# A graph network's edge stage on one core: raw edge features transposed two tiles at a time and split behind the transposes, with ScalarE's steps in another order

## What is computed

```python
ei = jnp.concatenate([x[src], edge_attr], axis=-1)          # 100000 x (256 + 64)
core = jnp.maximum(ei @ W1 + b1, 0.0) @ W2 + b2
gate = jax.nn.sigmoid(ei @ Wg + bg)
agg = jax.ops.segment_sum(gate * core, dst, num_segments=N)
out = agg + x
# layer norm of out; x = layernorm(x + out); then two hops of a normalised
# neighbour sum, a 256x256 product, log-softmax, and a last layer norm
```

## Time and profile before

| | us |
|---|---|
| median of 3 runs | 2623.61 (2621.59 to 2627.11) |
| the profiled execution | 2622.07 |
| its span, first to last instruction | 2620.1 |
| TensorE busy, share of the span | 2366.6, 90% |
| VectorE busy | 1906.3, 73% |
| ScalarE busy | 1638.6, 63% |
| GpSimd busy | 1417.6, 54% |

### The profile page before, as it was taken

One profiled execution on the slowest core, in us unless ns is written; L12 is line 12 of the kernel. 1 busy time (PEld: TensorE's weight loads), 2 busy tenths in 40 slices (PEclk: granted clock), 3 DMA queues, 4 the chain that ended last, 5 costly groups with the idle time before them and its releaser, 6 DMA issues. The chain is left out here.

```text
span 2620.1 us, 48396 instructions
## 1 busy us (share of the span) xinstructions
PE 2366.6 (90%) x16053; PEld 1842.6 (70%) x16053; DVE 1906.3 (73%) x4579; ACT 1638.6 (63%) x3119; POOL 1417.6 (54%) x1385
## 2 busy tenths in 40 slices
PE   7879999999999999999999994799999999888864
PEld 3469999999999999999999992255555444445443
DVE  6647777777777777888888999896777851435455
ACT  1158888888888888888888884464676630102123
POOL 0265555555555555555555641466666626666663
PEclk9989999999999999999999996899999999999986
DMA  6555555555555556556666652354565445565542
GB/s 209 194 182 166 167 164 164 164 164 164 164 166 163 165 164 179 174 163 180 179 179 181 179 152 82 86 147 130 134 170 149 114 141 192 183 217 191 168 131 87
DMA packets 276156, 422.40 MB, mean 161 GB/s; under 512 B 127618, under 2 KB 198548, under 8 KB 273860
## 3 DMA queue, kind: packets, MB, share of 16 engines
q0 software_dynamic: 90368, 281.11, 37.7%
q1 hardware_dynamic: 170028, 116.99, 14.6%
q10 hardware_dynamic: 15512, 21.17, 2.3%
HBM read 354.78 MB, written 64.37 MB: 160 GB/s over the span
## 5 line engine op out<-in xcount | busy, mean ns | idle before, releaser
L823 POOL DMA_INDIRECT gathered<-p_table,src_t x784 | 793.0, 1012 | 621.4 <-PE banks L965 431.6
L823 POOL DMA_INDIRECT gathered<-hop_table,src_t x576 | 591.5, 1027 | 437.4 <-issue 148.3
L988 PE MATMUL banks<-w_hi,hidden_hi 128*128 128x256 f32 x1568 | 458.0, 292 | 30.4 <-ACT banks L1327 29.6
L988 PE MATMUL banks<-w_lo,hidden_hi 128*128 128x256 f32 x1568 | 442.6, 282 | 0.0
L988 PE MATMUL banks<-w_hi,hidden_lo 128*128 128x256 f32 x1568 | 442.1, 282 | 0.0
L1440 ACT CAST counts<-banks 128x686 f32 (+3 forms) x382 | 295.5, 773 | 174.4 <-PE banks L1053 76.3
L1320 ACT CAST msg_hi<-room 128x512 fp32r<-128x512 f32 x392 | 242.1, 618 | 213.0 <-DVE room L1810 207.7
L1810 DVE TENSOR_TENSOR room<-banks,gate 128x512 f32<-128x512 f32 x392 | 255.9, 686 | 153.3 <-issue 122.9
L988 PEld LDWEIGHTS banks<-w_hi,hidden_hi 128*128 128x128 f32 x1568 | 297.6, 190 | 48.7 <-issue 38.1
L1800 DVE SCALAR_TENSOR_TENSOR hidden_lo<-banks,hidden_hi 128x512 fp32r<-128x512 f32 x392 | 268.7, 689 | 55.5 <-ACT hidden_hi L1313 32.8
L1050 PE MATMUL banks<-codes,low_hot 128*128 128x343 f16 (+3 forms) x958 | 240.3, 335 | 74.8 <-DVE codes L2026 47.9
(11 more groups left out here) (223 smaller groups left out, 5249.1 us busy)
## 6 DMA issues: line engine op xcount, KB each, us to landing
ea<-in_edge_attr SPq DMA_DIRECT2D x196, 128.0 KB
counts_saved<-counts SPq DMA_DIRECT2D x16, 1568.0 KB
ring<-counts_saved SPq DMA_DIRECT2D x16, 1568.0 KB
gathered<-p_table,src_t POOLq DMA_INDIRECT x784
p_table<-p_t ACTq DMA_DIRECT2D x48, 256.0 KB, 3.4
hop_table<-parts SPq DMA_DIRECT2D x12, 896.0 KB
gathered<-hop_table,src_t POOLq DMA_INDIRECT x576
x_saved<-x_room SPq DMA_DIRECT2D x7, 896.0 KB
```

What stands on the lines that cost most here:

```text
L823: pool.indirect_dma_start(out=rows[:, n % slots, j, :], out_offset=None, in_=table[:, :], in_offset=bass.IndirectOffsetOnAxis(ap=src_t[:, ...
L988: last = nc.tensor.matmul(banks[:, 4 + half, j % 2 * H:(j % 2 + 1) * H], lhs, rhs, start=False, stop=n == len(products) - 1, skip_group_ch ...
```

## The change

- TensorE transposes the raw features, two tiles side by side (2 x 64 columns), so two transposes for a group, not four. They wait for the load itself (`ea_loaded`). In bank 7, partitions 0 to 63 then hold tiles 0 and 2, partitions 64 to 127 tiles 1 and 3.
- ScalarE's `round_ea` and `copy_ea` go. `upper_ea(n+3)` makes the upper parts in two copies of 64 partitions x 256 out of the bank, and VectorE's `lower_ea`, now at lag 3, makes the lower parts in two subtractions of 64 x 256, out of the bank and into the 64 partitions opposite. It raises `ea_ready`.
- Tiles stand in another order in the transposed table (`turned_at`). `load_ea` waits for `ea_turned`, not for `ea_split`.
- ScalarE's order: open_gate goes from the end of the step to just behind upper_ea and the node rows, one group later (lag 1, not 2); seed_core is taken apart: half 0 stands between upper_msg half 0 and upper_hidden 0, half 1 closes the step.

```diff
+        def turned_at(j):
+            return slice((j % 2 * 2 + j // 2) * P, (j % 2 * 2 + j // 2 + 1) * P)
+        raw_halves = ((slice(0, DE), slice(0, 2 * P), slice(DE, P)), (slice(DE, P), slice(2 * P, GROUP), slice(0, DE)))
             def load_ea(i, s):
-                wait_count(sp, S["ea_split"], g - 1)
+                wait_count(sp, S["ea_turned"], g - 1)
             def turn_ea(turn, s, g):
-                pe.wait_ge(S["ea_split"], g + 1)
+                pe.wait_ge(S[f"ea_loaded{s}"], 16 * (turn + 1))
                 wait_count(pe, S["ea_ready"], g)
-                for j in range(TILES):
-                    last = nc.tensor.transpose(banks[:, 7, j * P:(j + 1) * P],
-                                               ea_split[:, s, j, :, :].bitcast(F32).rearrange("p b d -> p (b d)"), ident[:, :])
+                for j in range(TILES // 2):
+                    last = nc.tensor.transpose(banks[:, 7, j * P:(j + 1) * P], ea[:, s, 2 * j:2 * j + 2, :].rearrange("p b d -> p (b d)"), ident[:, :])
-            def round_ea(turn, s, g):
-                act.wait_ge(S[f"ea_loaded{s}"], 16 * (turn + 1))
-                wait_count(act, S["ea_turned"], g - 1)
-                nc.scalar.copy(ea_split[:, s, :, 0, :], ea[:, s, :, :]).then_inc(S["ea_rounded"], 1)
-            def copy_ea(turn, s, g):
+            def upper_ea(turn, s, g):
                 act.wait_ge(S["ea_turned"], g + 1)
                 wait_count(act, S["gate_product"], 2 * (g - 1))
-                nc.scalar.copy(ea_turned_sb[:, s, :], banks[:, 7, :]).then_inc(S["ea_ready"], 1)
+                for rows, columns, _ in raw_halves:
+                    nc.scalar.copy(ea_turned_sb[rows, s, columns], banks[rows, 7, 0:2 * P]).then_inc(
+                        S["ea_upper"], 1)
             def step(i, s, in_order=True):
-                at_group(copy_ea, i, s, 3)
-                at_group(round_ea, i, s, 5)
+                at_group(upper_ea, i, s, 3)
                 if in_order and isinstance(i, int):
                     node_rows_at(2 * i + s)
+                at_group(open_gate, i, s, 1)
                 at_group(seed_gate, i, s, 2)
                 at_group(upper_msg(0), i, s, 0)
+                at_group(seed_core(0), i, s, 1)
                 at_group(upper_hidden(0), i, s, 2)
                 at_group(upper_msg(1), i, s, 0)
                 at_group(upper_hidden(1), i, s, 2)
-                at_group(seed_core, i, s, 1)
-                at_group(open_gate, i, s, 2)
+                at_group(seed_core(1), i, s, 1)
             def lower_ea(turn, s, g):
-                dve.wait_ge(S["ea_rounded"], g + 1)
-                nc.vector.tensor_tensor(ea_split[:, s, :, 1, :], ea[:, s, :, :], ea_split[:, s, :, 0, :].bitcast(F32),
-                                        ALU.subtract).then_inc(S["ea_split"], 1)
+                for half, (rows, columns, others) in enumerate(raw_halves):
+                    dve.wait_ge(S["ea_upper"], 2 * g + half + 1)
+                    last = nc.vector.tensor_tensor(ea_turned_sb[others, s, columns], banks[rows, 7, 0:2 * P],
+                                                   ea_turned_sb[rows, s, columns].bitcast(F32), ALU.subtract)
+                last.then_inc(S["ea_ready"], 1)
...
-                at_group(lower_ea, i, s, 5)
+                at_group(lower_ea, i, s, 3)
```

More of the change, by code:

```diff
@@ L261, in gnn_kernel @@
         msg_hi = at("msg_hi", 91712, [P, STEP, HP], F32R)
-        ea_split = at("ea_split", 102784, [P, 2, TILES, 2, DE], F32R)
         p_t = at("p_t", 91712, [P, P_SLOTS, H2])
@@ L392, in gnn_kernel @@
         xa_turned xa_ready p_product p_ready banks_opened
-        ea_rounded ea_split ea_turned ea_ready hidden_product hidden_upper hidden_ready
+        ea_turned ea_upper ea_ready hidden_product hidden_upper hidden_ready
         gate_product gate_seeded gate_ready core_seeded core_done msg_ready msg_upper msg_split0 msg_split1 hot_ready scattered agg_added
@@ L964, in hidden_product @@
                     for j in range(TILES):
-                        last = nc.tensor.matmul(banks[:, k, j * P:(j + 1) * P], gathered[:, s, j, columns], ident[:, :],
+                        last = nc.tensor.matmul(banks[:, k, turned_at(j)], gathered[:, s, j, columns], ident[:, :],
                                                 start=False, stop=j == TILES - 1, is_transpose=True)
@@ L973, in gate_product @@
                     for j in range(2 * half, 2 * half + 2):
-                        to, lhs = banks[:, 2 + half, j % 2 * H:(j % 2 + 1) * H], ea_turned_sb[:, s, j * P:(j + 1) * P]
+                        to, lhs = banks[:, 2 + half, j % 2 * H:(j % 2 + 1) * H], ea_turned_sb[:, s, turned_at(j)]
                         nc.tensor.matmul(to, lhs, w_e_hi[:, H:H2], start=False, stop=False, skip_group_check=True)
@@ L984, in core_product @@
                     for j in range(2 * half, 2 * half + 2):
-                        products = [(a[s][k][:, j * P:(j + 1) * P], b[:, k, :]) for k in range(KC)
+                        products = [(a[s][k][:, turned_at(j)], b[:, k, :]) for k in range(KC)
                                     for a, b in ((hidden_hi, w_2_hi), (hidden_hi, w_2_lo), (hidden_lo, w_2_hi))]
@@ L1321, in upper_msg, with seed_core, stage @@
                 return stage
-            def seed_core(turn, s, g):
-                for half in range(2):
+            def seed_core(half):
+                def stage(turn, s, g):
                     wait_count(act, S["msg_ready"], 2 * g + half - 1)
@@ L1328, in seed_core @@
                                    bias_core.unsqueeze(1).to_broadcast([P, 2, H])).then_inc(S["core_seeded"], 1)
+                return stage
             def open_gate(turn, s, g):
```

## The result

The changed kernel takes **2669.7 us** (median of 4 runs, 2666.9 to 2674.0) against 2625.4 for the kernel before in the same comparison: 1.0163, with an interval of 1.0141 to 1.0185. The forecast was 2595, a gain. This is the page of the changed kernel.

The account below looks back on a forecast made before the run. TensorE's chain (7.00 us issue plus about 0.24 hole) bounds; afterwards VectorE's ring, 5.82 + 0.50 + 0.33 + 0.27 = 6.92. Stretch differences sum to -28.8 on 2622.1: 2593.3, plus 1.5 for the median: 2595 us, range 2560 to 2617.

Parts of the forecast that it names:

- The hole: TensorE's idle time ahead of a core product, waiting for ScalarE's bias copy: about 0.24 us a step.
- TensorE's floor, 6.78: TensorE's pure issue a step: two transposes less save 0.22 us, from 7.00 to 6.78.
- Hole gone by seed 0: Seed_core's first half, placed earlier on ScalarE, cuts its core-product chain to 6.0 us, well under 6.78.
- Seed 1 the late one, 6.7: Seed_core's second half, wanted half a core product later, becomes the late one: chain 6.7 us, just under 6.78.
- open_gate, the longer load: Moving open_gate on ScalarE is covered, thinly with node rows; the load with twice the bytes costs nothing.
- ScalarE's net -0.2: On ScalarE, two PSUM copies at about 0.28 us replace copy_ea (0.46) and round_ea (0.31): net -0.2.
- VectorE's ring: VectorE's chain from one message to the next: 5.82 us before, 6.92 after, becoming the bound.
- the three joints: Where VectorE instructions follow one another around lower_ea's halves: changed partitions lose the overlap, 0.09 us each, 0.27 together.
- Stretches two to five: Later parts of the edge stage, with node work added on VectorE: steps of 6.94, 7.05, 7.21 and 7.65 us.
- Overlap kept: Rival 1: VectorE's instructions around lower_ea still overlap, 6.66 us, below TensorE's 6.78; 2560 us, chance 0.24.
- Hole stays: Rival 2: something else releases TensorE's idle time; only 0.22 us gained in the first three stretches; 2607 us, chance 0.14.
- Halves dear: Rival 3: crossing partitions makes lower_ea's two subtractions costlier; at 0.60 us each 2663 us, chance 0.09.

Follow-up runs that it names:

- e2: Kernel before with only seed_core taken apart, half 0 ahead of upper_hidden 0, half 1 behind upper_hidden 1: 2609.0 us, ratio 0.9937.
- e7: e2 with only the first two of four transposes from group 1 on (output not the reference's): 2474.5 us, ratio 0.9947 to the kernel before.
- e6: Changed kernel with lower_ea ahead of lower_hidden 0, turn_ea behind core products, upper_ea behind seed_gate, add_window behind lower_msg: 2460.6 us, ratio 0.9894 to kernel before.
- e8: e2 with open_gate moved to the next step, ahead of seed_gate: 2500.4 us, ratio 1.0050 to the kernel before.
- e4: Changed kernel with add_window moved behind lower_msg in VectorE's step: 2631.8 us, ratio 1.0028 to the kernel before.
- e3: Changed kernel with both lower_ea subtractions reading and writing partitions 0 to 63 (output not the reference's): 2611.6 us, ratio 0.9950 to kernel before.
- g1: The kernel of e6, run again on another chip: 2573.2 us, ratio 0.9876 to the kernel before on that chip.

## Why the prediction was wrong

**What bounds the kernel before: right, for chip A.** The hole, its releaser and its size stand: e2 moves half a seed and the step falls from 7.24 to 7.02 and 7.00. That it belongs to the chip as much as to the kernel could not be read from one trace.

**TensorE's floor, 6.78: right** (e7, e6). **Hole gone by seed 0: right** (e2). **Seed 1 the late one, 6.7: right in kind.** The wait at the second half is there, in the changed kernel [the waits above], but behind messages that are already late.

**open_gate, the longer load: nothing, right** (e8; e6 reaches the floor with the same load). **ScalarE's net -0.2: it is nothing, and without effect.** The two copies take 0.39 each to the next start, not 0.28 (below), 0.78 for the 0.77 of copy_ea and round_ea.

**The bound moves to VectorE's ring: right. Its size, 6.92: the failed step.** It is 7.23. Term by term, medians of start to start in the first stretch:

| | forecast | measured |
|---|---|---|
| message to second lower_hidden, seed included | 3.38 | 3.40 |
| second lower_hidden to additions | 0.61 | 0.84 |
| two additions | 0.80 | 0.79 |
| lower_msg, joint included | 1.29 | 1.31 |
| two halves of lower_ea, joints included | 0.84 | 0.89 |
| sum | 6.92 | 7.23 |

Of the 0.31, 0.23 is one term: the start after lower_hidden was taken as if the next instruction could start at once. The rows stood in the prediction: 907.71 to 908.55 is 0.84, and the sum entered 0.61. The ring of before was thus 6.05, not 5.82. e4 confirms it: with the additions elsewhere, 0.24 comes back. The other 0.07 are the three joints, where the loss is not only the overlap of 0.09 but 0.01 to 0.04 more.

Both terms are small, but there was no slack under them: before, a ring of 6.05 left 0.95 us to TensorE's 7.00, and the change spends 0.52 on the seed and 0.67 on lower_ea. At 7.23 the ring takes back on A all that the hole gave (7.24), and on C, where there is no hole, it costs 0.22 from the first step (7.22 against 6.99).

**Stretches two to five.** Forecast 6.94, 7.05, 7.21 and 7.65, measured 7.12, 7.44, 7.66 and 8.38. e4 says what the place of the additions is worth: 0.24 us a step in the first stretch, 0.06, 0.09 and 0.01 in the next three, where only every second step has additions, and 0.43 in the fifth, where the fetch of the row number takes up to 1.20 us. That is 36 of the 75 us by which the forecast was off. The 0.07 of the joints, if it holds in all 195 steps, is 13 more. What is left lies in the third to fifth stretches, some 0.2, 0.4 and 0.2 us a step. The forecast took node work there from VectorE's busy time. Busy time leaves out the pauses between short instructions that need one another, as the two at 1398.02 and 1398.21. That this is the cause of the rest was not tested.

**The rivals.** Overlap kept: e3 is that kernel, 2611.6, so even then VectorE's ring (6.89) and not the 6.78 would have been the bound. Hole stays: no, the first stretch's 7.23 looks like it, but VectorE never waits for TensorE there. Halves dear: it named 2663 us, near the 2670 measured, and for the wrong reason. The halves are 0.43 long and 0.43 apart, not 0.60. The forecast gave slower 0.09, since all its slower cases hung on that one price; the ring's other terms were taken as exact. Two small sums of the prediction are off and change nothing: the steps at 0.48 a half add up to -5, not -7 (2618 in place of 2617), and 0.73 + 5 x 0.50 is 3.23, not 3.25.

## What to carry to other kernels

Where a change moves the bound to another engine's ring, add that ring up from measured starts of the same pair of instructions, and check the sum against the whole ring in the trace of before; a term taken from another pair hides what the sequencer does between. Put work of an engine where it waits anyway: with the same subtractions at the end of VectorE's step the step is 6.99 us, the sum of VectorE's ring (e4, on A), ahead of lower_hidden it is TensorE's 6.78 (e6, on B and C; 6.96 on D). And a stall of a few tenths of a microsecond that waits for a signal may be a matter of the chip: time both kernels on more than one before a gain of 1% is believed.

## What was not expected of the hardware

- **TensorE's signals come late on some chips.** In the kernel before, medians from 300 to 720 us, the first half of a core product signals 1.8 us and the second 0.95 us later on A than on C; on D the transposes of g1 signal 0.9 us later than those of e6 on B. The instructions are the same, and where no hole stands the step on A is the 7.00 us of C. On D the signals of the core product's second half, of the transposes behind it and of the first hidden product come within 0.12 us of each other (437.48, 437.52, 437.60), on B 0.2 and 0.9 apart (462.66, 462.88, 463.78). The kernel before takes 2604 to 2625 us on A and D and 2487 on B and C. Of the 135 us between the profiled spans on A and C, 44 are in the edge stage (1412.6 and 1368.3 us), nearly all the rest behind it; that the rest has the same cause was not shown. What holds the signals was not found, and as B, C and D were each timed on one occasion only, it is not shown either that it is the chip and not the time.
- **ScalarE seems to lose its overlap too when the partitions change.** Of the two copies of 64 x 256 in the changed kernel the first starts at partition 0, as what stands ahead of it, and overlaps it by 0.08 us. The second starts at partition 64: it is 0.37 us long and starts 0.39 behind the first, and the sigmoid at partition 0 starts 0.39 behind it, both without an overlap. Copies that stay on the same partitions start 0.08 to 0.14 before the one ahead ends (L1299 of before: 0.44 long, 0.31 to the next start). No run changes this alone.
- **A row number that VectorE's queue fetches costs 0.23 us** where one instruction stands ahead of it in the first stretch, and nothing where two do (e4).
